# Transposed probabilities: four tiles in one round trip through the scratch tensor instead of two tiles in each of two

## The chip, the cores and the metric

The kernel runs on one core of one Trainium2 chip. The metric is the device time of one execution in microseconds. Three runs of the kernel before gave a median of 2397.24 us (2396.45 to 2406.7). Besides these there is one profiled execution with its trace.

Engines are named as in the profile: PE is TensorE (PEld its weight loads), DVE is VectorE, ACT is ScalarE, POOL is GpSimd, SP is SyncE, which here issues every DMA.

## The reference

The reference is a decoder of two layers on 16 sequences of 64 tokens with 512 features, in float32: self attention, cross attention and a feed-forward part per layer, each with a residual and a layer norm behind it. Three of these six parts are 32-head attentions with 8 key/value heads of size 128, and only they are touched by the change. Cut to what matters (the masks differ; the third takes keys and values from the context and normalises queries and keys by their root mean square):

```python
qg = q.reshape(B, Hkv, G, N, D)                       # G = 4 query heads share one key head
s = einsum('bhgnd,bhmd->bhgnm', qg, k) * scale + bias # 64 x 64 scores per sequence and head
p = softmax(s, axis=-1)
o = einsum('bhgnm,bhmd->bhgnd', p, v)                 # needs p with its keys on the partitions
x = layernorm(x + o.reshape(B, N, Hq * D) @ wo.T)
```

The other parts (a small linear cross attention, a feed-forward part with int4 weights, a mixture of low-rank experts) stay as they are.

## The kernel before

The 1024 tokens are 8 tiles of 128 rows (two sequences each). All matrix products are made in three passes, from a high and a low part of each operand (`mm3`, L263 to L265), so every tensor that goes into TensorE is split in two: ScalarE or GpSimd writes the high part, VectorE or GpSimd subtracts to get the low part.

`pe_attention` and its namesakes for the other engines run the three 32-head attentions as three stages, `attn0` (roughly the first 565 us of the profile), `attn1` (from 1123 us) and `xattn1` (up to 2353 us, the one with `rms`). A stage is a loop over the 8 key/value heads i. In each turn TensorE projects queries, keys and values of head i (12 units, `U_0` to `U_11`) and in between works off the attention of head i - 1. The order is a list of words written out by hand in `schedule` (L65); every engine walks the same list and does its own share of each word. A minus behind a word means the head before. The words:

- `U_n`: a projection unit, 12 matmuls of 512 columns on TensorE, its bank emptied by ScalarE (in `xattn1` VectorE copies key and value units, L777 and L778, and normalises keys, L789).
- `SC` scores of one pair of tiles, with the softmax on VectorE and ScalarE; GpSimd multiplies by the reciprocal sums (L961). A head has 4 such pairs, so 4 times 128 x 512 probabilities in `sc_sb`.
- `TR` transposes: VectorE turns the probabilities of one pair in blocks of 32 x 32 (L843) into `pq[:, pair % 2]`. The blocks themselves still have to change places between partitions. That is done by DMA: `move_out` (L461) writes `pq` in 4 pieces of 64 KB to the DRAM tensor `turned[pair % 2]`, `move_in` (L466) reads it back in one transfer of 256 KB to `pt[:, pair % 2]`.
- `PT` splits the result: ScalarE `pth` (L729), VectorE `ptl` (L868). Both wait for `move_in`, ScalarE directly.
- `PV` multiplies it with the values on TensorE (L608); ScalarE makes `oth` (L733) and VectorE `otl` (L874).
- `WS` splits a chunk of the output weights (ScalarE `woh` L740, VectorE `wol` L883), `WO` projects a tile of the output with them (12 matmuls) and VectorE adds it to `X` (L880). The first `WO` of a head needs the four chunks one after the other, one per group of three matmuls.
- `KT` and `SQ` (`xattn1` only) transpose the normalised keys (L586) and sum squares of queries.

An engine's instructions run in the order of its program, so a wait holds everything behind it on that engine. SyncE is such an engine too: in `sp_attention`, `step` issues for each head six loads of projection weights (`load_w`, into five slots of `raw`, each as soon as the slot's last content is split: for c = 0 to 3 that is WS of chunk c), four loads of output weights (`load_o`) and, between them at fixed places, `move_out` and `move_in` of pairs 2 and 3 of the head before and of pairs 0 and 1 of this head. GpSimd splits the projection weights (L945, L947) and in `xattn1` the values (L954, L956).

After the last head comes a tail, the list in the branch `if not project` (L76), without projections to fill in; there the layer norm begins.

## Time and profile before

| | |
|---|---|
| median of three runs | 2397.24 us (2396.45 to 2406.7) |
| profiled execution | 2401.77 us |
| its span, first to last instruction | 2400.0 us |
| granted TensorE clock, mean | 0.973 of full speed |
| PE busy | 2289.1 us, 95% |
| DVE, ACT, POOL busy | 1206.0, 780.5, 765.6 us |
| VectorE transposes (L843) | 96, mean 704 ns |
| DMA | 152.43 MB, mean 64 GB/s |

The busy times say which engine is close to being full, not what a change is worth: for that one has to read, in the stretch where the change lies, which wait ended last before TensorE went on. Starts in a timeline are in microseconds from the first instruction. The starts and ends of matmuls overlap, since they are pipelined; what matters is the distance from start to start. `x4` behind a row means that four like instructions stand in it, one behind the other.

### The profile page before, as it was taken

How to read it: one execution, taken by the hardware profiler on the slowest of the kernel's cores; microseconds unless marked ns; L12 is line 12 of the kernel's file. 1: busy time of each engine (PE TensorE's matmuls, PEld its weight loads, DVE VectorE, ACT ScalarE, POOL GpSimd, SP SyncE). 2: the span in 40 equal slices, each digit the busy share in tenths (PEclk: the TensorE clock that was granted, in tenths of full speed). 3: DMA queues.
4: the chain of work that ended last, by engine and by line, in shares of the span. 5: the costliest groups of instructions: out<-in, count | busy, mean ns of one | idle time of the engine just before them, and what ended most of it. 6: DMA issues, size and time to landing. Idle time of an engine off the chain costs nothing. (4 is left out here: it accounts for less than half of the span.)

```text
span 2400.0 us, 34599 instructions
## 1 busy us (share of the span) xinstructions
PE 2289.1 (95%) x12210; PEld 1833.6 (76%) x12210; DVE 1206.0 (50%) x2052; ACT 780.5 (33%) x1475; POOL 765.6 (32%) x709
## 2 busy tenths in 40 slices
PE   8999999997999989998999999998899999999989
PEld 6888888875555557886788888887788888888867
DVE  3445544447677633334444444556345454544456
ACT  2233223223677731222322223332232233323321
POOL 4122222203333335444222222211443433333233
PEclk9999999998999999999999999999889999999989
DMA  4222222211000113311221222121121212211120
GB/s 160 80 66 60 76 79 79 57 45 32 18 18 11 64 70 123 105 52 54 81 80 50 67 75 78 56 53 49 59 80 54 57 48 79 67 43 53 53 75 36
DMA packets 120546, 152.43 MB, mean 64 GB/s; under 512 B 16272, under 2 KB 67984, under 8 KB 119952
## 3 DMA queue, kind: packets, MB, share of 16 engines
q1 hardware_dynamic: 120464, 151.33, 21.5%
q8 instruction: 52, 0.85, 0.1%
q14 instruction: 30, 0.25, 0.0%
HBM read 124.02 MB, written 27.26 MB: 63 GB/s over the span
## 5 line engine op out<-in xcount | busy, mean ns | idle before, releaser
L263 PE MATMUL banks<-xTh,wh 128*128 128x512 f32 x1024 | 418.7, 409 | 8.8 <-DVE xTl L1887 7.4
L265 PE MATMUL banks<-xTh,wl 128*128 128x512 f32 x1024 | 404.7, 395 | 0.0
L264 PE MATMUL banks<-xTl,wh 128*128 128x512 f32 x1024 | 403.6, 394 | 0.0
L263 PE MATMUL banks<-woh,oth 128*128 128x512 f32 x768 | 315.6, 411 | 23.3 <-DVE otl L874 16.4
L264 PE MATMUL banks<-wol,oth 128*128 128x512 f32 x768 | 302.5, 394 | 0.0
L961 POOL TENSOR_TENSOR sc_sb<-sc_sb,rs 128x512 f32<-128x512 f32 x96 | 104.3, 1090 | 621.1 <-DVE rs L837 621.1
L265 PE MATMUL banks<-woh,otl 128*128 128x512 f32 x768 | 302.1, 393 | 0.0
L880 DVE TENSOR_TENSOR X<-banks,X 128x512 f32<-128x512 f32 x192 | 132.7, 691 | 324.3 <-PE banks L265 323.9
L693 ACT ACTIVATE q_sb<-banks 128x512 f32<-128x512 f32 x192 | 114.5, 597 | 400.6 <-PE banks L265 400.6
L263 PEld LDWEIGHTS banks<-xTh,wh 128*128 128x128 f32 x1024 | 195.6, 191 | 51.0 <-issue 9.2
L265 PEld LDWEIGHTS banks<-xTh,wl 128*128 128x128 f32 x1024 | 194.9, 190 | 44.0
L264 PEld LDWEIGHTS banks<-xTl,wh 128*128 128x128 f32 x1024 | 195.9, 191 | 37.3
L564 PEld LDWEIGHTS banks<-k_sb,q_sb 128*128 128x128 f32 x1536 | 191.0, 198 | 19.0 <-ACT q_sb L693 6.7
L874 DVE TENSOR_TENSOR otl<-banks,oth 128x512 fp32r<-128x512 f32 x192 | 123.6, 686 | 158.6 <-ACT oth L733 158.6
L564 PE MATMUL banks<-k_sb,q_sb 128*128 128x64 f32 x1536 | 191.4, 279 | 9.5 <-ACT q_sb L693 4.1
L263 PEld LDWEIGHTS banks<-woh,oth 128*128 128x128 f32 x768 | 146.2, 190 | 69.3 <-DVE otl L874 17.9
L947 POOL TENSOR_TENSOR wl<-raw,wh 128x512 fp32r<-128x512 f32 x144 | 193.4, 1343 | 12.0
L945 POOL TENSOR_SCALAR wh<-raw 128x512 fp32r<-128x512 f32 x144 | 91.0, 632 | 314.1 <-DMA raw<-in_a_in 163.7
L265 PEld LDWEIGHTS banks<-woh,otl 128*128 128x128 f32 x768 | 145.9, 190 | 32.4
L264 PEld LDWEIGHTS banks<-wol,oth 128*128 128x128 f32 x768 | 146.4, 191 | 26.3
L733 ACT ACTIVATE oth<-banks 128x512 fp32r<-128x512 f32 x192 | 104.3, 596 | 124.1 <-PE banks L608 124.1
L690 ACT ACTIVATE sq<-banks 128x512 f32<-128x512 f32 x64 | 38.3, 598 | 242.7 <-PE banks L265 242.7
(208 smaller groups left out, 4039.9 us busy)
## 6 DMA issues: line engine op xcount, KB each, us to landing
raw<-in_a_in SPq DMA_DIRECT2D x144, 256.0 KB, 2.9
raw<-in_a_out SPq DMA_DIRECT2D x96, 256.0 KB, 2.7
turned<-pq SPq DMA_DIRECT2D x384, 64.0 KB, 2.0
pt<-turned SPq DMA_DIRECT2D x96, 256.0 KB, 2.9
f_q<-in_f_q SPq DMA_DIRECT2D x21, 512.0 KB, 3.9
f_s<-in_f_s SPq DMA_DIRECT2D x21, 512.0 KB, 5.3
X<-in_x SPq DMA_DIRECT2D x1, 2048.0 KB, 10.5
x_craw<-in_ctx SPq DMA_DIRECT2D x8, 256.0 KB, 2.7
```

The costliest lines, as they stand in the source:

```text
L263: nc.tensor.matmul(out, w_hi, x_hi, start=start, stop=False)
L264: nc.tensor.matmul(out, w_hi, x_lo, start=False, stop=False)
L265: return nc.tensor.matmul(out, w_lo, x_hi, start=False, stop=stop)
L564: last = nc.tensor.matmul(pb[2][:, (4 * c + m) * S:(4 * c + m + 1) * S], q_sb[:, 4 * (pair % 2) + m, c * P:(c + 1) * P], k_sb[:, col:col + S],
L690: nc.scalar.activation(sq[:, :, g % 2 * S:(g % 2 + 1) * S], bank[:, :].rearrange("p (c s) -> p c s", c=8), ACT.Square).then_inc(A["q_sq"], 1)
L693: nc.scalar.activation(q_sb[:, :, g * S:(g + 1) * S], bank[:, :].rearrange("p (c s) -> p c s", c=8), ACT.Copy).then_inc(A["q_free" if st.r ...
L733: nc.scalar.activation(oth[:, n % 2, :, 64 * b:64 * b + 64], PVB[b][:, :].rearrange("p (c s) -> p c s", c=8), ACT.Copy).then_inc(A["o_hi"], 1)
L874: nc.vector.tensor_tensor(otl[:, n % 2, :, half], PVB[b][:, :].rearrange("p (c s) -> p c s", c=8), f32(oth[:, n % 2, :, half]), ALU.subtra ...
L880: nc.vector.tensor_tensor(xtile(n), bank[:, :], xtile(n), ALU.add).then_inc(A["x_added"], 1)
L945: nc.gpsimd.tensor_scalar(hi, src, 1.0, 0.0, ALU.mult, ALU.add).then_inc(A["w_hi"], 1)
L947: nc.gpsimd.tensor_tensor(lo, src, f32(hi), ALU.subtract).then_inc(A["w_ready"], 1)
L961: nc.gpsimd.tensor_tensor(rows, rows, spread_rows(rs[:, pair, :]), ALU.mult).then_inc(A["p_ready"], 1)
```

## The change

Pairs 0 and 1 now travel together, as half 0, and pairs 2 and 3 as half 1.

- `TR0` and `TR2` leave the lists; `TR1` and `TR3` make both transposes of their half back to back and then count once on `t_done`.
- `move_out` writes both buffers of `pq` in 4 pieces of 128 KB; `move_in` reads 512 KB into both buffers of `pt`.
- For half 1 SyncE issues `move_out` behind `load_w` 2 (before: behind `load_w` 1 for pair 2 and behind `load_w` 3 for pair 3) and `move_in` behind `load_w` 4 (before: behind 2 and 4). For half 0 `move_out` stands behind `load_o` 1 (`xattn1`: 2) and `move_in` one place further.
- One semaphore each instead of two for the pieces and for the return.

```diff
--- before.py
+++ after.py
@@ -68,13 +68,13 @@
 
 
     if rms:
-        ev = events("U_0 PT0- TR2- U_1 WS0- WS1- U_2 PV0- PT1- TR3- WS2- WS3- U_3 WO0- PV1- U_4 KT0 PT2- WO1- U_5 KT1 PV2- WO2- SQ0 "
-                    "U_6 PT3- U_7 WO3- SQ1 PV3- SC0 WO4- SC1 U_8 U_9 WO5- SQ2 TR0 U_10 U_11 TR1 WO6- SQ3 SC2 WO7- SC3")
+        ev = events("U_0 PT0- U_1 WS0- WS1- U_2 PV0- PT1- TR3- WS2- WS3- U_3 WO0- PV1- U_4 KT0 PT2- WO1- U_5 KT1 PV2- WO2- SQ0 "
+                    "U_6 PT3- U_7 WO3- SQ1 PV3- SC0 WO4- SC1 U_8 U_9 WO5- SQ2 U_10 U_11 TR1 WO6- SQ3 SC2 WO7- SC3")
     else:
-        ev = events("U_0 VT1- PT0- TR2- U_1 WS0- WS1- U_2 PV0- PT1- TR3- WS2- WS3- U_3 WO0- PV1- U_4 PT2- WO1- U_5 PV2- WO2- SC0 "
-                    "PT3- WO3- SC1 U_6 PV3- WO4- U_7 WO5- U_8 TR0 WO6- U_9 TR1 WO7- SC2 U_10 SC3 U_11 VT0")
+        ev = events("U_0 VT1- PT0- U_1 WS0- WS1- U_2 PV0- PT1- TR3- WS2- WS3- U_3 WO0- PV1- U_4 PT2- WO1- U_5 PV2- WO2- SC0 "
+                    "PT3- WO3- SC1 U_6 PV3- WO4- U_7 WO5- U_8 WO6- U_9 TR1 WO7- SC2 U_10 SC3 U_11 VT0")
     if not project:
-        return events("PT0- TR2- PV0- WO6-- " + ("" if rms else "VT1- ") + "PT1- TR3- WO7-- WS0- WS1- PV1- WS2- WS3- WO0- PT2- WO1- "
+        return events("PT0- PV0- WO6-- " + ("" if rms else "VT1- ") + "PT1- TR3- WO7-- WS0- WS1- PV1- WS2- WS3- WO0- PT2- WO1- "
                       "PV2- WO2- PT3- WO3- PV3- WO4- WO5- WO6- WO7-")
     if project == "last":
         return [e for e in ev if e[0] != "WO" or e[1] < 6]
@@ -293,7 +293,7 @@
         names = dict(
             proj_done=96, proj_free=96, sc_done=32,
             s_out=32, s_max=32, s_sub=32, exp_done=32, s_sum=32, s_rec=32, p_ready=32,
-            t_done=32, pt_hi=32, pt_ready=32,
+            t_done=16, pt_hi=32, pt_ready=32,
             pv_done=32, o_hi=64, o_ready=64,
             wo_done=64, x_added=64,
             wo_hi=32, wo_ready=32,
@@ -307,8 +307,8 @@
         ld_w = [sem(f"ld_w{c}") for c in range(6)]
         ld_o = [sem(f"ld_o{c}") for c in range(4)]
         ld_b = sem("ld_b")
-        pt_in = [sem(f"pt_in{n}") for n in range(2)]
-        pq_out = [sem(f"pq_out{n}") for n in range(2)]
+        pt_in = sem("pt_in")
+        pq_out = sem("pq_out")
         turned = nc.dram_tensor("turned", (2, P, 512), F32, kind="Internal").ap()
 
         xs = {n: sem("x_" + n) for n in (
@@ -419,7 +419,7 @@
 
         def pt_wait(eng, st, i, pair, more):
 
-            wait(eng, pt_in[pair % 2], 16 * (16 * st.index + 2 * i + pair // 2 + more))
+            wait(eng, pt_in, 16 * (16 * st.index + 2 * i + pair // 2 + more))
 
         def input_quarter(n):
 
@@ -454,16 +454,16 @@
                         sp.dma_start(bias[r, :, :], src.rearrange("p (c g s) -> p c g s", c=2, g=2)[:, :, h, :]
                                      ).then_inc(ld_b, 16)
 
-            def move_out(i, pair):
-                st.need(sp, "t_done", 4 * i + pair + 1)
-                rows = turned[pair % 2].rearrange("(bk j) (q n) -> q j bk n", bk=4, q=4)
+            def move_out(i, half):
+                st.need(sp, "t_done", 2 * i + half + 1)
+                rows = turned.rearrange("t (bk j) (q n) -> q j (t bk) n", bk=4, q=4)
                 for q in range(4):
-                    sp.dma_start(rows[q], pq[32 * q:32 * q + 32, pair % 2, :].rearrange("j (bk n) -> j bk n", bk=4)
-                                 ).then_inc(pq_out[pair % 2], 16)
-
-            def move_in(i, pair):
-                wait(sp, pq_out[pair % 2], 64 * (16 * st.index + 2 * i + pair // 2 + 1))
-                sp.dma_start(pt[:, pair % 2, :], turned[pair % 2]).then_inc(pt_in[pair % 2], 16)
+                    sp.dma_start(rows[q], pq[32 * q:32 * q + 32, :, :].rearrange("j t (bk n) -> j (t bk) n", bk=4)
+                                 ).then_inc(pq_out, 16)
+
+            def move_in(i, half):
+                wait(sp, pq_out, 64 * (16 * st.index + 2 * i + half + 1))
+                sp.dma_start(pt[:, :, :], turned.rearrange("t p n -> p t n")).then_inc(pt_in, 16)
 
             if st.before:
                 sp.wait_ge(*stage_end(st.before))
@@ -491,7 +491,7 @@
 
             def step(i, before, more):
 
-                first, second = (1, 2) if st.rms else (0, 1)
+                second = 2 if st.rms else 1
                 for c in range(5):
                     if more:
                         if c < 4:
@@ -499,20 +499,20 @@
                         else:
                             st.need(sp, "w_ready", 6 * i + 6)
                         load_w(i + 1, c, c)
-                    if before and c in (1, 3):
-                        move_out(i - 1, 2 + c // 2)
-                    if before and c in (2, 4):
-                        move_in(i - 1, 1 + c // 2)
+                    if before and c == 2:
+                        move_out(i - 1, 1)
+                    if before and c == 4:
+                        move_in(i - 1, 1)
                 for c in range(4):
                     if more:
                         st.need(sp, "w_ready", 6 * (i + 1) + c + 1)
                     else:
                         st.need(sp, "wo_ready", 4 * (i - 1) + c + 1)
                     load_o(i, c, c)
-                    if c in (second, second + 1):
-                        move_in(i, c - second)
-                    if c in (first, second):
-                        move_out(i, c - first)
+                    if c == second + 1:
+                        move_in(i, 0)
+                    if c == second:
+                        move_out(i, 0)
                 if more:
                     load_bias(i + 1)
                     st.need(sp, "w_ready", 6 * (i + 1) + 5)
@@ -522,9 +522,8 @@
             with sp.Fori(1, NKV - 1) as i:
                 step(i, True, True)
             step(NKV - 1, True, False)
-            for pair in (2, 3):
-                move_out(NKV - 1, pair)
-                move_in(NKV - 1, pair)
+            move_out(NKV - 1, 1)
+            move_in(NKV - 1, 1)
 
 
         def pe_attention(pe, st):
@@ -806,7 +805,7 @@
                 rows = sc_sb[:, pair, :, :]
                 b = bias[:, :, :].rearrange("p c (o s) -> p c o s", o=1).to_broadcast([P, 2, 4, S])
                 st.need(dve, "sc_done", 4 * i + pair + 1)
-                st.need(dve, "t_done", 4 * (i - 1) + pair + 1)
+                st.need(dve, "t_done", 2 * (i - 1) + pair // 2 + 1)
                 if st.per_head_bias:
                     dve.wait_ge(ld_b, 32 * (i + 2))
                 else:
@@ -836,13 +835,16 @@
                 st.need(dve, "s_sum", 4 * i + pair + 1)
                 nc.vector.reciprocal(rs[:, pair, :], ssum[:, pair, :]).then_inc(A["s_rec"], 1)
 
-            def transpose_probs(i, pair):
-
-                st.need(dve, "p_ready", 4 * i + pair + 1)
-                pt_wait(dve, st, i, pair, 0)
-                nc.vector.transpose(pq[:, pair % 2, :].rearrange("p (bk ct i) -> p ct bk i", bk=4, i=32),
-                                    sc_sb[:, pair, :, :].rearrange("p c s -> p (c s)").rearrange(
-                                        "p (ct bk i) -> p ct bk i", bk=4, i=32)).then_inc(A["t_done"], 1)
+            def transpose_probs(i, half):
+
+                pt_wait(dve, st, i, 2 * half, 0)
+                for n in range(2):
+                    pair = 2 * half + n
+                    st.need(dve, "p_ready", 4 * i + pair + 1)
+                    last = nc.vector.transpose(pq[:, n, :].rearrange("p (bk ct i) -> p ct bk i", bk=4, i=32),
+                                               sc_sb[:, pair, :, :].rearrange("p c s -> p (c s)").rearrange(
+                                                   "p (ct bk i) -> p ct bk i", bk=4, i=32))
+                last.then_inc(A["t_done"], 1)
 
             def run(i, events):
                 for kind, n, age in events:
@@ -862,7 +864,7 @@
                     elif kind == "SU":
                         sums(j, n)
                     elif kind == "TR":
-                        transpose_probs(j, n)
+                        transpose_probs(j, n // 2)
                     elif kind == "PT":
                         st.need(dve, "pt_hi", 4 * j + n + 1)
                         nc.vector.tensor_tensor(ptl[:, :], pt[:, n % 2, :], f32(pth[:, :]),
```

## Rows read from the trace of the kernel before

**Rows 1.** The page, busy us, share of the span and instructions of each engine.
```profile
PE 2289.1 (95%) x12210; PEld 1833.6 (76%) x12210; DVE 1206.0 (50%) x2052; ACT 780.5 (33%) x1475; POOL 765.6 (32%) x709
```

**Rows 2.** Windows of steady heads, stages one and three: stretch, length, busy us, clock.
```profile
100.00:510.00 410.00, 409.93 (x2183) 338.24 (x2182) 191.72 (x327) 113.71 (x205) 91.03 (x91) 1.00 0.24 67
...
1836.00:2240.00 404.00, 389.94 (x2451) 340.46 (x2450) 204.86 (x396) 120.83 (x277) 145.83 (x141) 1.00 0.21 59
```

**Rows 3.** TensorE's waits, whole kernel: us in total, times, longest.
```profile
PE banks L263 <- DVE otl L874: 16.4, 7, 2.8
...
PE banks L608 <- DVE ptl L868: 14.1, 5, 5.5
```

**Rows 4.** The page's DMA issues: count, KB each, median us from issue to landing.
```profile
turned<-pq SPq DMA_DIRECT2D x384, 64.0 KB, 2.0
...
pt<-turned SPq DMA_DIRECT2D x96, 256.0 KB, 2.9
...
f_q<-in_f_q SPq DMA_DIRECT2D x21, 512.0 KB, 3.9
...
f_s<-in_f_s SPq DMA_DIRECT2D x21, 512.0 KB, 5.3
```

**Rows 5.** Timeline of VectorE, stage one: start, duration, line, tiles.
```profile
336.72 0.70 DVE L843 STREAM_TRANSPOSE pq<-sc_sb 128x512 f32<-128x512 f32 x1
...
345.27 0.69 DVE L868 TENSOR_TENSOR ptl<-pt,pth 128x512 fp32r<-128x512 f32 x1 [2.17 <-ACT pth L729]
```

**Rows 6.** Timeline of VectorE, 337.5 to 338.2 us: WS2 alone.
```profile
337.35 1.16 DVE L883 TENSOR_TENSOR wol<-raw,woh 128x512 fp32r<-128x512 f32 x1
```

**Rows 7.** Timeline of GpSimd, 335 to 339 us.
```profile
336.21 1.74 POOL L947 TENSOR_TENSOR wl<-raw,wh 128x512 fp32r<-128x512 f32 x1
```

**Rows 8.** Timeline of TensorE, 338 to 350 us: third group of WO0, and PV2.
```profile
338.16 0.39 PE L265 MATMUL banks<-woh,otl 128*128 128x512 f32 x1
...
338.56 0.50 PE L263 MATMUL banks<-woh,oth 128*128 128x512 f32 x1
...
349.45 0.39 PE L608 MATMUL banks<-pth,vh 64*128 64x256 f32 x2
```

**Rows 9.** Timeline of SyncE's DMA issues, 338 to 345 us.
```profile
338.67 0.36 SPq L440 DMA_DIRECT2D raw<-in_a_in  x1
...
340.16 1.93 SPq L461 DMA_DIRECT2D turned<-pq  x4
...
344.08 0.34 SPq L466 DMA_DIRECT2D pt<-turned  x1
```

**Rows 10.** Timeline of ScalarE, 344 to 346 us.
```profile
344.61 0.62 ACT L729 ACTIVATE pth<-pt 128x512 fp32r<-128x512 f32 x1
```

**Rows 11.** Timeline of VectorE, stage three.
```profile
1847.25 0.70 DVE L843 STREAM_TRANSPOSE pq<-sc_sb 128x512 f32<-128x512 f32 x1
...
1856.24 1.25 DVE L883 TENSOR_TENSOR wol<-raw,woh 128x512 fp32r<-128x512 f32 x2
...
1866.28 0.98 DVE L789 TENSOR_SCALAR kst<-kst,rk 128x128 f32<-128x128 f32 x2
```

**Rows 12.** Timeline of TensorE, 1852 to 1869 us.
```profile
1855.15 0.50 PE L263 MATMUL banks<-woh,oth 128*128 128x512 f32 x1 [2.77 <-DVE otl L874]
...
1856.95 0.50 PE L263 MATMUL banks<-woh,oth 128*128 128x512 f32 x1
...
1868.20 0.60 PE L586 MATMUL banks<-ident,kst 128*128 128x128 f32 x4
```

**Rows 13.** Timeline of GpSimd, 1861 to 1869 us.
```profile
1867.27 1.28 POOL L956 TENSOR_TENSOR vl<-vst,vh 128x512 fp32r<-128x512 f32 x1
```

**Rows 14.** Timeline of SyncE's DMA issues, 1857 to 1865 us.
```profile
1857.06 0.36 SPq L440 DMA_DIRECT2D raw<-in_a_in  x1
```

**Rows 15.** Timeline of SyncE's DMA issues, tail of stage one.
```profile
539.16 0.34 SPq L466 DMA_DIRECT2D pt<-turned  x1
```

**Rows 16.** Timeline of VectorE, tail of stage one.
```profile
544.19 0.68 DVE L868 TENSOR_TENSOR ptl<-pt,pth 128x512 fp32r<-128x512 f32 x1
```

## The prediction

> **What bounds the kernel now.** I read the page's busy lines first, then TensorE's waits, then the busy time of two stretches, then the timelines around one head. TensorE is busy 2289.1 us, 95% [rows 1]. In the steady heads of the first attention stage it has nothing to give back: 409.93 of 410 us busy, and the second stage is the same program with the same picture. In the steady heads of the third, 14 of 404 us are idle [rows 2], before L263 on `otl` (16.4 us in 7 waits in the whole kernel) [rows 3]. So the transfers that the change merges are no bound; what counts is whether the new order makes TensorE wait. Waits on `ptl`, the far end of the changed chain, cost it 14.1 us in 5 places, with 5.5 the longest [rows 3], all in the tails of the stages, where few projections are left to fill in. SyncE, which issues the 384 pieces out and the 96 returns [rows 4], waits for events most of the time, so half of these issues gone buys nothing by itself.
>
> **Part 1, the second transpose in front of the weight split (first two stages).** TR2 stood after PT0, where VectorE next waits for ScalarE; taken out there, it gives TensorE nothing. It now runs behind TR3, and right behind that stands WS2. A transpose starts 0.63 us before what follows it (336.72 to 337.35) [rows 5, 6]. WS2 starts at 337.35 and takes 1.16 us, where two of its kind take 1.25 together in the third stage [rows 6, 11]. It ends as late as 338.51 because L947 on GpSimd runs until 337.95 beside it, for 1.74 us instead of the 1.28 of L956, which does the same work on another tile [rows 7, 13]. The transpose at 336.72 took its 0.70 us beside that L947 too, and I take the second one to do the same. It then fills the wait that WS2 has anyway: WS2 starts at 337.98, with L947 gone, takes 0.68 and ends at 338.66, 0.15 us later. TensorE already waits there: the third L263 of that output projection starts 0.40 us after a matmul of 0.39, though matmuls overlap elsewhere, and 0.05 us behind the end of WS2 [rows 8]. So 0.15 us is exposed in full. 11 heads of the two stages stand like this (0 to 5, without the very first, whose WO0 comes later): 1.7 us. Head 6 of each stage has no L947 beside it; there WS2 would end without delay at about 338.03 by this head's clock, and 0.61 later is 0.1 to 0.3 past its need, with 0.1 for the slower first matmul behind a wait (0.50 instead of 0.39): 0.7 us for the two. Bounds: 0 (the second transpose hidden) and 13 times 0.61, 7.9 us.
>
> Weighed beside it: the Trainium skill, "SBUF — State Buffer", Who interferes with whom, says that a VectorE instruction with two SBUF inputs and a GpSimd one that reads SBUF exclude each other wholly, and that one with a single SBUF input, outside the two-port modes, does not contend. By this rule, the trace agrees: 1.16 and 1.74 us are an undisturbed one and 0.46 to 0.5 each, and the transpose keeps its 0.70. Without the rule part 1 would be 7.9 us, with it 2.4.
>
> **Part 2, the same move in the third stage.** Here VectorE is in the chain. TR2 (1847.25) is followed back to back by the copies of the next projection unit, these by ScalarE's squares, WS0 and WS1, the next copies, and `otl` of PV0, for which TensorE waits 2.77 us before it starts WO0 at 1855.15 [rows 11, 12]. Without TR2 this comes 0.62 us earlier. But then follow `ptl`, two transposes instead of one, and WS2: its first half starts at 1856.24 again, and the third L263, at 1856.95 behind it today, stays there. Minus 0.62 and plus 0.62: 0. Bounds: minus 4.3 us (7 heads by 0.62, if WS2 did not hold the third L263) and plus 4.3.
>
> **Part 3, PT2 gets its data later.** Today PT2 (`pth` on ScalarE, 344.61) [rows 10] is not held by its data; they have been there for over 2 us. Now the pieces of pairs 2 and 3 leave together behind load_w 2, which waits for WS2. That load was issued 0.16 us behind WS2's end, at 338.67; now 338.82, and the first piece 0.4 later, behind the load's own 0.36: 339.22. From the first piece of pair 3 to the issue of its return passed 3.92 us (340.16 to 344.08) for 256 KB [rows 9]. Another 256 KB add 1.0, the difference of `f_q`'s 512 KB, landed after 3.9, and the return's 256 KB, landed after 2.9 [rows 4]. So the merged return is issued at 344.14; with `f_q`'s 3.9 it lands at 348.04. `pth` and `ptl` need 1.35 us (344.61 to 345.96) [rows 5, 10]: 349.39. TensorE comes to PV2 at 349.45 [rows 8], plus part 1's 0.15: 349.60. It is hidden, with 0.2 us to spare. Bounds: a landing 2.9 or 5.3 us (`f_s`) after issue, that is 1.2 to spare or 1.2 late; late counts in 12 heads. Behind PT2 on VectorE stands the X addition of WO1, needed by WO2 behind the whole of PV2: covered; on ScalarE nothing is due before U_5 ends.
>
> In the third stage: load_w at 1857.06 [rows 14], first piece 1857.46, return 1862.38, landed 1866.3 (1865.3 to 1867.7). PV2 comes behind L586 and is covered. But behind PT2 and the addition on VectorE stand the two L789 that normalise the last keys, today done at 1867.26; TensorE's transposes of these keys (L586) start at 1868.20, 0.9 us in hand [rows 11, 12]. `pth` would end at 1866.9, `ptl` at 1867.6 or a little after, the addition 0.6 later, and L789 meets L956 on GpSimd, which starts at 1867.27 and runs 1.28 us [rows 13]. Today the two L789, of 128x128 each, need 0.98 us beside other work of GpSimd, so they would be held until L956 ends. With the earliest landing the keys are ready near 1868.95, 0.75 late, with 1866.3 near 1869.55, 1.35 late. I take 1.0 us in 6 heads (0 to 5; head 6 has neither the loads in front nor GpSimd beside it): 6.0 us. Bounds 0 and 2.0 each, 12.
>
> **Part 4, the rest.** TR0 beside TR1: those pairs are read only in the next head, behind a further 10 us and more of projections; nothing there is late. The tails: the pieces leave right behind the transposes, 0.6 later than today. The return, today issued at 539.16 [rows 15], goes out near 540.3 with the larger pieces and lands at 544.2. `pth` and `ptl` then end near 545.5 instead of 544.87 [rows 16], and PV2, with a little in hand today, starts some 0.4 late: 0.8 us for the two tails of this kind; in the third stage the data come earlier against their reader. Bounds 0 and 3.
>
> **Sum.** 1.7 + 0.7 + 0 + 0 + 6.0 + 0.8 = 9.2 us. The profiled execution took 2401.77 us for a span of 2400.0, so it would take 2411.0; it lies 4.5 us above the median of 2397.24, and against that median the change gives 2406.4.
>
> **Rivals.**
> A, the slower side: PV2 waits for the merged return in the first two stages. It decides from a landing later than 348.2, 4.1 us behind its issue. For it: the return follows two 256 KB loads (load_w 3 and 4) and 512 KB in 512-byte rows into the same queue, and `f_s` took 5.3. Against it: `f_q` at 3.9, and the smaller returns, which land in 2.9 behind a load as well. Price: at 5.3 us 1.2 late in 12 heads, 14 us, and 1.8 in the third stage instead of 1.0, 5 us: 2425.
> B, no wait for the keys: L789 goes in before L956, or the return lands 1.5 us sooner. For it: the gap in which VectorE finds GpSimd between two instructions. Against: `ptl`, the addition and L789 would have to fit before 1867.27. 2406.4 - 6.0 = 2400.4.
> C, faster: the 0.62 us is gained at WO0 in the third stage and WS2 does not take it back, with B as well: 2396.1. Against: the third L263 starts right behind WS2 now, and WS2's own chain does not get shorter.
> That the transfers are not merged as said gets nothing: they are plain copies of strided rows.
>
> **Chances.** Forecast 0.48, A 0.27, B 0.20, C 0.05. A measurement of this kernel tells 0.5% from no change, 12 us: 2385 and 2409. Slower: A and the upper end of the forecast (0.06), 0.33. Faster: 0.03, what C may hide. Same: 0.64. The range goes from C to A: 2395 to 2425.
>
> **What the changed profile would show.** In a steady head of the first stages WS2 is about 0.7 us long and the third L263 waits 0.15 more; if 0.6, part 1 is four times its price. In the third stage the wait before WO0 falls from 2.8 to 2.2 us and the one at the third L263 grows by as much. The return is issued 5 us behind its first piece and lands 3.9 later; L586 waits for L789, 0.7 to 1.4 us, six times. A wait of L608 on `ptl` in steady heads would be rival A. A steady head that gets shorter would make the whole wrong.

## Result, and the profile after

The changed kernel takes 2429.53 us, the median of four runs (2424.98 to 2439.92), against 2396.84 (2395.8 to 2406.7) for the kernel before: a ratio of 1.0126, 95% interval 1.0097 to 1.0155. The forecast was 2406.4 us, with a range up to 2425; the kernel is slower than that. Ratios here and below are worked out over all runs of either kernel, so they differ a little from the quotient of the medians. The profiled execution took 2428.49 us for a span of 2426.7, 26.7 more than before. Its mean granted clock was 0.970 of full speed, before 0.973.

The busy line of the page (busy time, share of the span, instructions), which answers to [rows 1]:

```profile
PE 2299.8 (95%) x12210; PEld 1838.8 (76%) x12210; DVE 1199.7 (49%) x2052; ACT 783.8 (32%) x1475; POOL 763.7 (31%) x709
```

TensorE did the same 12210 matmuls and was busy 10.7 us longer, though no matmul was added; the other 16 us of the 26.7 are idle time. What ended its idle time (us in all, number of waits, the longest), which answers to [rows 3]:

```profile
PE banks L607 <- DVE ptl L870: 19.4, 13, 5.5
PE banks L263 <- DVE otl L876: 12.6, 7, 2.2
PE banks L263 <- DVE wol L885: 9.7, 14, 0.7
PE banks L585 <- DVE kst L788: 6.2, 6, 1.5
PE banks L354 <- DVE X L346: 4.1, 4, 1.9
```

Waits on `ptl` were 5 and are 13. Six waits on `kst`, the keys, are new, and so are most of those on `wol`: 6 waits of 3.9 us together before. The first matmul behind a wait is slower as well, so the growths given below are up to 0.16 us larger per wait than the idle time: 7.2 us for the keys, where these lines have 6.2. The transfers themselves are merged as the diff says (count, KB each, median us from issue to landing; before in [rows 4]):

```profile
turned<-pq SPq DMA_DIRECT2D x192, 128.0 KB, 2.5
pt<-turned SPq DMA_DIRECT2D x48, 512.0 KB, 3.8
```

**Where the 26.7 us are.** I set the start of each of the 12210 matmuls of one trace against its counterpart in the other, and read the growth of the distance from place to place. The first attention stage holds 2.0, the second 6.1, the third 17.0; what lies between and behind them gives 1.0 back; the first 36 us, where the first weights are loaded, cost 2.6, and a second profile of the kernel before has 3.3 there as well, so that is taken as chance. By kind, in us (growth at a matmul that runs at another clock in one of the two traces is the clock's, growth at one behind another wait is the wait's):

| | predicted | in the two profiles |
|---|---|---|
| third L263 of WO0, first two stages | 2.4 | 2.1 |
| WO0 in the third stage | 0 | 0.4 |
| PV2 waits for the data, steady heads | 0 | 4.2 |
| keys (L585) in the third stage | 6.0 | 7.2 |
| tails | 0.8 | 4.0 |
| TensorE at half clock in the third stage | not in the sum | 6.3 |
| start; between and behind the stages; the rest of the stages | 0 | 2.6 - 1.0 + 0.9 |

The half clock: added up over the third attention stage, the clock was granted at half speed for 64.9 us instead of 51.2. In the steady heads 2 to 6 of that stage (stretch, length, then busy time and count of PE, PEld, DVE, ACT, POOL, then the granted clock, DMA share and GB/s), before:

```profile
1839.50:2232.00 392.50, 378.44 (x2363) 329.31 (x2362) 196.30 (x380) 117.81 (x270) 144.78 (x140) 1.00 0.22 60
```

and after:

```profile
1849.40:2255.90 406.50, 387.64 (x2362) 335.53 (x2361) 195.80 (x380) 119.38 (x270) 143.66 (x140) 0.98 0.21 58
```

Five heads are 14.0 us longer. 4.8 us of that is idle time of PE (18.9 instead of 14.1), 9.2 is busy time with the same matmuls, most of it because the clock falls four times (a fall is a stretch of half clock; they last 3.4 or 6.8 us here). Such a fall, and an undisturbed stretch close to it, in the kernel after:

```profile
1897.90:1901.30 3.40, 3.40 (x14) 3.01 (x14) 2.59 (x5) 0.13 (x1) 1.94 (x3) 0.50 0.00 0
1890.90:1894.30 3.40, 3.40 (x18) 2.81 (x17) 0.32 (x1) 1.09 (x2) 0.00 (x0) 1.00 0.00 0
```

TensorE is busy through both and waits for nobody, but in the first it runs at 0.50, that is 1.2 instead of 2.4 GHz. A list of waits does not show this at all; only the clock column does.

**One head, as the prediction went through it.** SyncE in the head of [rows 9] (start, duration, instruction), in the kernel after:

```profile
342.19 0.33 SPq L440 DMA_DIRECT2D raw<-in_a_in  x1
342.67 1.98 SPq L461 DMA_DIRECT2D turned<-pq  x4
344.90 1.27 SPq L440 DMA_DIRECT2D raw<-in_a_in  x2
347.25 0.38 SPq L466 DMA_DIRECT2D pt<-turned  x1
```

This head lies 3 us later than before. The return goes out 4.58 us behind the first piece, where the prediction had 4.92. On VectorE, the last subtraction of PT1, the two transposes and WS2 with WS3:

```profile
339.56 0.68 DVE L870 TENSOR_TENSOR ptl<-pt,pth 128x512 fp32r<-128x512 f32 x1
340.16 1.30 DVE L844 STREAM_TRANSPOSE pq<-sc_sb 128x512 f32<-128x512 f32 x2
341.38 1.25 DVE L885 TENSOR_TENSOR wol<-raw,woh 128x512 fp32r<-128x512 f32 x2
```

WS2 no longer meets GpSimd: two of its kind take 1.25 us together, where one took 1.16 [rows 6]. That is the cover that part 1 counted on. The reader of the returned data is ScalarE:

```profile
351.28 0.63 ACT L728 ACTIVATE pth<-pt 128x512 fp32r<-128x512 f32 x1 [3.00 <-DMA pt<-turned]
```

It starts when the transfer has landed, 4.0 us behind its issue, after 3.0 us of waiting. `ptl` is ready about 352.6, and PV2 starts at 353.01: this head escapes by 0.4 us. Others don't. Over the 24 heads the return of half 1 lands 3.4 to 5.3 us behind its issue, median 4.05, and in the first two stages PV2 waits in seven steady heads (3.7 us of waits, 4.2 with the slower matmuls behind them), for instance:

```profile
285.29 0.39 PE L607 MATMUL banks<-pth,vh 64*128 64x256 f32 x2 [0.40 <-DVE ptl L870]
```

In the third stage the keys, TensorE first, then VectorE:

```profile
1879.77 0.65 PE L585 MATMUL banks<-ident,kst 128*128 128x128 f32 x4 [1.51 <-DVE kst L788]
```

```profile
1877.95 0.70 DVE L870 TENSOR_TENSOR ptl<-pt,pth 128x512 fp32r<-128x512 f32 x1 [6.15 <-ACT pth L728]
1878.57 0.68 DVE L882 TENSOR_TENSOR X<-banks,X 128x512 f32<-128x512 f32 x1
1879.17 0.47 DVE L788 TENSOR_SCALAR kst<-kst,rk 128x128 f32<-128x128 f32 x2
```

VectorE stands 6.15 us idle in front of `ptl`, the last link behind the transfer, and the two normalisations that TensorE waits for are queued behind it though their own data were there. In this head the return landed 5.3 us behind its issue. In two others of the six it was `ptl` that took long, beside GpSimd's `vl` (L958, 2038.10 to 2039.39):

```profile
2038.19 1.75 DVE L870 TENSOR_TENSOR ptl<-pt,pth 128x512 fp32r<-128x512 f32 x1 [5.09 <-ACT pth L728]
```

These three waits are 1.4 to 1.5 us. In the other three the first normalisation took 0.71 us and ended with GpSimd's L958, and TensorE waited 0.5 to 0.7.

The third stage's tail has a path of its own. Behind the last return SyncE issues the loads for the next part of the decoder (`g_raw`). The first of them goes out 12.5 us after PV0's start in that tail and lands 4.3 us behind its issue; in the kernel before these were 11.1 and 3.0 us. GpSimd waits for it, and only when it has split these weights does it make `rstd`, the root of the layer norm. VectorE's L346 now waits for `rstd`, and did not before:

```profile
2350.48 0.41 SPq L1676 DMA_DIRECT2D g_raw<-in_g_gate  x1
```

```profile
2354.83 1.05 POOL L1691 TENSOR_SCALAR g_h<-g_raw 128x552 fp32r<-128x552 f32 x1 [15.96 <-DMA g_raw<-in_g_gate]
```

```profile
2359.86 0.84 DVE L346 TENSOR_SCALAR X<-X,mv,rstd 128x512 f32<-128x512 f32 x1 [2.37 <-POOL rstd L341]
```

### The profile page after: what moved, and what is told of

It is laid out like the page before. It is cut to its first block and busy times, and to the rows that moved or that the text cites. A ratio compares the mean times of both kernels' runs of the same rounds, so it can differ in the third digit from the quotient of the medians.

```text
span 2426.7 us, 34327 instructions
## 1 busy us (share of the span) xinstructions
PE 2299.8 (95%) x12210; PEld 1838.8 (76%) x12210; DVE 1199.7 (49%) x2052; ACT 783.8 (32%) x1475; POOL 763.7 (31%) x709
## 3 DMA queue, kind: packets, MB, share of 16 engines
q1 hardware_dynamic: 116624, 151.32, 20.6%
## 5 line engine op out<-in xcount | busy, mean ns | idle before, releaser
L263 PE MATMUL banks<-xTh,wh 128*128 128x512 f32 x1024 | 418.0, 408 | 9.5 <-DVE xTl L1889 8.0
L263 PE MATMUL banks<-woh,oth 128*128 128x512 f32 x768 | 318.7, 415 | 25.5 <-DVE otl L876 12.6
L263 PEld LDWEIGHTS banks<-xTh,wh 128*128 128x128 f32 x1024 | 194.8, 190 | 52.3 <-issue 9.3
L563 PEld LDWEIGHTS banks<-k_sb,q_sb 128*128 128x128 f32 x1536 | 196.6, 203 | 18.5 <-ACT q_sb L692 6.7
L563 PE MATMUL banks<-k_sb,q_sb 128*128 128x64 f32 x1536 | 197.3, 285 | 8.9 <-ACT q_sb L692 4.1
L263 PEld LDWEIGHTS banks<-woh,oth 128*128 128x128 f32 x768 | 147.7, 192 | 72.8 <-DVE wol L885 19.4
L947 POOL TENSOR_SCALAR wh<-raw 128x512 fp32r<-128x512 f32 x144 | 90.9, 631 | 314.3 <-DMA raw<-in_a_in 164.5
L870 DVE TENSOR_TENSOR ptl<-pt,pth 128x512 fp32r<-128x512 f32 x96 | 71.9, 749 | 151.5 <-ACT pth L728 151.5
## 6 DMA issues: line engine op xcount, KB each, us to landing
X<-in_x SPq DMA_DIRECT2D x1, 2048.0 KB, 10.4
```

The lines of the kernel that those rows point to most:

```text
L263: nc.tensor.matmul(out, w_hi, x_hi, start=start, stop=False)
L563: last = nc.tensor.matmul(pb[2][:, (4 * c + m) * S:(4 * c + m + 1) * S], q_sb[:, 4 * (pair % 2) + m, c * P:(c + 1) * P], k_sb[:, col:col + S],
L870: nc.vector.tensor_tensor(ptl[:, :], pt[:, n % 2, :], f32(pth[:, :]), ALU.subtract).then_inc(A["pt_ready"], 1)
L947: nc.gpsimd.tensor_scalar(hi, src, 1.0, 0.0, ALU.mult, ALU.add).then_inc(A["w_hi"], 1)
```

## Experiments

### Which half of the change costs the time

**e1_dma_only.** The transfers of after with the transposes where they stood before; `move_out` waits for both of its half.

```diff
-                st.need(sp, "t_done", 2 * i + half + 1)
+                st.need(sp, "t_done", 4 * i + 2 * half + 2)
```

> Transfers merged as in the changed kernel, but the four transposes stay at their old places in the lists (TR2 behind PT0, TR0 behind U_8), so only SyncE's part of the change is made. Theory R (the merged return of pairs 2 and 3 comes late): the waits of L608 on ptl in steady heads and of the key transposes on L789 stay as in the changed kernel, 5 to 6 us and about 7 us, with the stretches at half clock in the third stage; only the 2 us in front of WS2 go, about 2427. Theory T (the loss comes from two transposes in a row on VectorE): within 3 us of before, about 2398.

Measured: 2423.54 us against 2398.65, ratio 1.0089 (1.0063 to 1.0115). The waits show the two mechanisms of the merged return (PV2 and the keys), with `wol` near what it was, and `otl` too (16.8 us):

```profile
PE banks L607 <- DVE ptl L867: 17.8, 9, 5.5
PE banks L585 <- DVE kst L788: 5.4, 6, 1.5
PE banks L263 <- DVE wol L882: 4.7, 8, 0.7
```

**e2_tr_only.** The other half: transposes in couples, transfers per pair as before.

```diff
+                        transpose_probs(j, n - 1)
                         transpose_probs(j, n)
```

> Transposes two by two at TR1 and TR3 as in the changed kernel, transfers per pair (64 KB pieces, 256 KB returns) at the places of before. Theory R: only the wait of WO0's third group on wol is longer, 2 us in all, no wait for the keys: about 2399. Theory T: nearly the whole loss, 2420 or more.

Measured: 2403.85 us, ratio 1.0013 (0.9998 to 1.0028).

```profile
PE banks L608 <- DVE ptl L869: 13.7, 4, 5.5
PE banks L263 <- DVE wol L884: 9.0, 13, 0.7
```

There are no waits for the keys and none of PV2 in steady heads. `wol` grows as in part 1 and in the third stage, where `otl` falls by as much (12.3 us instead of 16.4). The wait on `X` at L354 in the third tail grows too, from 1.9 to 5.2 us in all, without a merged transfer: here as well the loads of `g_raw` go out later, 15.1 us after PV0's start in that tail instead of 11.1. So the transposes cost a few us at most; most of the loss is in the transfers.

**e3_half0_only.** Only pairs 0 and 1 travel together, transposes and transfers; half 1 as before.

```diff
-                    if c in (second, second + 1):
-                        move_in(i, c - second)
-                    if c in (first, second):
-                        move_out(i, c - first)
+                    if c == second + 1:
+                        in_pairs(i)
+                    if c == second:
+                        out_pairs(i)
...
+                        if n == 1:
+                            transpose_probs(j, 0)
```

(`out_pairs` sends 4 pieces of 128 KB, `in_pairs` brings 512 KB back.)

> Only pairs 0 and 1 merged (transposes and transfers), pairs 2 and 3 as before. Theory R: no change, 2397 within 3 us, since the reader of half 0 comes 9 us and more after its landing. A rival by which merging costs wherever it is done (longer use of the queue in front of the weight loads): a loss of a third or more, 2407 and up.

Measured: 2401.58 us, ratio 1.0001 (0.9985 to 1.0018). Half 0 costs nothing that can be measured, as the forecast had it. The loss is in half 1.

### Which wait of half 1

**e4_keys_first.** After, but in the third stage VectorE does `ptl` of PT2 behind the keys instead of ahead of them.

```diff
+        if st.rms and project and ("PT", 2, 1) in both:
+            both.remove(("PT", 2, 1))
+            both.insert(both.index(("U_", 5, 0)) + 1, ("PT", 2, 1))
```

> The changed kernel with one thing moved: in the third stage VectorE does the low part ptl of PT2 behind the copies and key normalisation of U_5, so that the keys no longer stand behind the return. Theory R with the clock as its consequence: the 7.2 us of waits before the key transposes go, and with them the half-clock stretches added in the third stage (13.7 us of them, worth 6.3 us), a wait of PV2 on ptl of 0 to 0.3 us per head in their place: 12 us below the changed kernel, about 2417. If the half-clock stretches have another cause, only 6 to 7 us below it, about 2423.

Measured: 2415.06 us against 2398.65, ratio 1.0073 (1.0044 to 1.0101). No wait at L585 is left, `ptl` waits are

```profile
PE banks L607 <- DVE ptl L870: 19.9, 18, 5.5
```

and the third stage is at half clock for 41 us instead of 64.9. The median is 14 us under that of after (9 to 13 by the ratios, against either set of runs of after), where the key waits were 7: that speaks for a slower clock that comes with them. The four runs spread from 2406.6 to 2422.6, and the profile is the fastest of them, so its 41 us are the low end; e7 tests the same from the other side.

**e5_out_first.** After, with the pieces of half 1 sent ahead of `load_w` 2.

```diff
-                    if before and c == 2:
+                    if before and c == 1:
                         move_out(i - 1, 1)
```

> The changed kernel, but SyncE issues the pieces of pairs 2 and 3 in front of load_w 2 instead of behind it, so they leave when the transposes end and do not wait for WS2. Theory R (lateness of the return in front of its reader): pieces and return about 1.2 us earlier; the steady waits of L608 on ptl (5.6 us) nearly all go, the waits for the keys (7.2 us) fall to 4 or 5, since L789 is still held by GpSimd's L956. About 2418. If the queue's load decides instead (the same bytes in the same stretch), the return lands no earlier and nothing changes, 2429.

Measured: 2417.39 us against 2398.77, ratio 1.0081 (1.0061 to 1.0101). SyncE, and ScalarE's reader, in the head shown above:

```profile
338.94 1.85 SPq L461 DMA_DIRECT2D turned<-pq  x4
341.05 1.58 SPq L440 DMA_DIRECT2D raw<-in_a_in  x3
343.04 0.38 SPq L466 DMA_DIRECT2D pt<-turned  x1
```

```profile
347.97 0.63 ACT L728 ACTIVATE pth<-pt 128x512 fp32r<-128x512 f32 x1 [2.27 <-DMA pt<-turned]
```

The pieces leave as the transposes end, and the return is out 1.7 us sooner by this head's clock. But three loads of 256 KB now stand right in front of it, and it takes 4.9 us instead of 4.0 to land: half the gain is lost in the queue. The PV2 waits of steady heads are gone, those of the keys are 2.8 us (a growth of 3.6): they are all of the kind that ends with GpSimd's L958.

**e6_split_return.** After, with the return in two transfers of 256 KB; PT2 waits for the first alone.

```diff
-                sp.dma_start(pt[:, :, :], turned.rearrange("t p n -> p t n")).then_inc(pt_in, 16)
+                for n in range(2):
+                    sp.dma_start(pt[:, n, :], turned[n]).then_inc(pt_in[n], 16)
```

> The changed kernel, but the return of 512 KB is two returns of 256 KB with a semaphore each, issued one behind the other at the same place; PT2 needs only the first. Theory R with the size of the return as its cause: the first half lands 1 us or more sooner, the steady waits of L608 on ptl fall below 1.5 us (from 5.6), those for the keys to about 5: 2421. If the place of the return is all that counts, no change, 2429.

Measured: 2419.31 us, ratio 1.0088 (1.0073 to 1.0103). The first return lands 3.3 us behind its issue in the median (2.7 to 4.1).

```profile
PE banks L608 <- DVE ptl L872: 13.7, 4, 5.5
PE banks L586 <- DVE kst L789: 4.3, 6, 1.5
```

What the size of the return costs is PV2's waits, which are gone from the steady heads; the keys stay late, by less: five of the six waits are 0.5 to 0.6 us, held by GpSimd.

**e7_key_wait_alone.** The kernel before, with nothing of the change, and the wait for the keys made by work: two spare subtractions on VectorE ahead of `ptl` of PT2 in the third stage.

```diff
+                            for k in range(2):
+                                nc.vector.tensor_tensor(spare[:, k, :], pt[:, 0, :], f32(pth[:, :]), ALU.subtract)
```

> The kernel before, with transfers and transposes untouched; in the third stage VectorE makes two further subtractions of 128x512 into a spare tile in front of the ptl of PT2, except in the tail, which pushes the key normalisation L789 back by 1.3 us, as the late return does. It is there to see whether the clock follows such waits. If waits before the key transposes (expected: 6 of about 0.9 us, 5 us) bring half-clock stretches with them, the third stage has 60 us or more of them instead of 51 and the kernel is 8 to 12 us slower than before, 2407. If the half clock has another cause, 5 us slower, 2402, with 41 to 51 us of it.

Measured: 2419.01 us, ratio 1.0095 (1.0075 to 1.0116).

```profile
PE banks L587 <- DVE kst L790: 7.8, 6, 1.3
```

8.7 us of added waits (7.8 of idle time and the slower matmuls behind it) cost 20.2 us in the median. In its profile, the fastest of the four runs, the half clock of the third stage is 68.3 us and costs 7.3. So the key wait alone brings the clock's part too, without a merged transfer.

**e10_three_mends.** After with e4, e5 and e6 together.

```diff
-                    if before and c == 2:
+                    if before and c == 1:
...
+                for n in range(2):
+                    sp.dma_start(pt[:, n, :], turned[n]).then_inc(pt_in[n], 16)
...
+                    both.insert(both.index(("U_", 5, 0)) + 1, ("PT", 2, 1))
```

> The changed kernel with the three mends together: pieces of pairs 2 and 3 issued in front of load_w 2, the return in two halves, and ptl of PT2 behind the key normalisation in the third stage. Theory R: no steady wait on ptl and none for the keys; what is left is the 2 us in front of WS2 and 1 to 3 us in the tails, about 2400. If more than 6 us remain above before, the change has a further cost not found yet.

Measured: 2407.57 us against 2403.84, ratio 1.0014 (0.9995 to 1.0032).

```profile
PE banks L608 <- DVE ptl L872: 15.4, 9, 5.5
PE banks L263 <- DVE wol L887: 10.5, 20, 0.7
```

No key wait, 44 us of half clock. With the three places mended the change is no different from before that can be measured: they carry the loss. It is no gain either; the waits on `wol` and in the third tail are still there.

### Is it the clock

**v1_order.** Meant as a gain: the kernel before, in the third stage TR2 behind U_2 and TR3 behind WS3.

```diff
-U_0 PT0- TR2- U_1 WS0- WS1- U_2 PV0- PT1- TR3- WS2- WS3- U_3
+U_0 PT0- U_1 WS0- WS1- U_2 TR2- PV0- PT1- WS2- WS3- TR3- U_3
```

> The kernel before with only its order of the third stage changed: TR2 behind the copies of U_2 (VectorE is idle there for 1.29 us) instead of behind PT0, and TR3 behind WS3 instead of in front of WS2. By the reading of the chain of VectorE the wait before WO0 shrinks by 0.6 us and that before its third group by 0.3 to 0.4 in 7 heads, 6 to 7 us in all: 2391. If TensorE waits for ScalarE's oth in any case, no change.

Measured: 2417.84 us against 2398.77, ratio 1.0079 (1.0063 to 1.0094): 19 us slower. Its waits fell as meant, before WO0

```profile
PE banks L263 <- DVE otl L874: 12.1, 6, 2.2
```

from 16.4 [rows 3], 5.9 us less in all with those at the third L263. A head without a fall would take 77.6 us (an estimate: the 78.5 of before less 0.85; none of heads 2 to 6 is without one). But heads 2 to 6:

```profile
1836.40:2239.60 403.20, 392.79 (x2362) 342.36 (x2362) 195.40 (x380) 118.26 (x270) 145.55 (x140) 0.96 0.22 59
```

Idle time 10.4 us instead of 14.1, and the clock 0.96 instead of 1.00: seven falls, 34 us of half clock there. Less waiting, more time. This profile, too, is the fastest of its six runs.

**e8_pad_06.** The kernel before with one short spare reduction on VectorE in each head of the third stage, ahead of `otl` of PV0, to make the wait before WO0 0.6 us longer.

```diff
+                                for k in range(1):
+                                    nc.vector.tensor_reduce(spare[:, k, :], PVB[0][:, :].rearrange("p (c s) -> p c s", c=8), AX_X, ALU.max)
```

> The kernel before, with one further reduction of 128x512 on VectorE in front of the otl of PV0 in the third stage, which makes the wait before WO0 and so each head about 0.6 us longer (79.1 instead of 78.5 us) and touches nothing else. Theory C (which weak stretches of a head lose the clock depends on the length of a head; at 78.5 us heads 2 to 6 go free): falls of the clock reappear in heads 2 to 6, two or more, 4 us of waits plus 6 us or more of half clock, about 2409. Theory W (the clock falls where waits get longer, in proportion): 4.3 us and a little more, 2402 to 2404.

Measured: 2429.94 us against 2403.84, ratio 1.0093 (1.0063 to 1.0123).

```profile
PE banks L264 <- DVE otl L878: 20.6, 7, 3.4
```

```profile
1835.70:2261.60 425.90, 409.25 (x2363) 353.44 (x2362) 200.42 (x386) 118.67 (x271) 143.92 (x140) 0.92 0.20 56
```

4.2 us more of waits, 26 us in the median. In each of the heads 2 to 6 the clock falls three times, 15 falls, 68 us of half clock; its third stage pays some 23 us more than that of before for matmuls at half clock. Each of the five waits before WO0, now 3.2 to 3.5 us, is followed by a fall at once. What a fall looks like from inside, TensorE behind the wait before WO0 (start, duration):

```profile
1852.03 0.50 PE L264 MATMUL banks<-woh,oth 128*128 128x512 f32 x1 [3.45 <-DVE otl L878]
1852.61 0.45 PE L266 MATMUL banks<-woh,otl 128*128 128x512 f32 x1
1852.85 0.63 PE L264 MATMUL banks<-woh,oth 128*128 128x512 f32 x1
1853.27 0.63 PE L265 MATMUL banks<-wol,oth 128*128 128x512 f32 x1
1853.70 0.63 PE L266 MATMUL banks<-woh,otl 128*128 128x512 f32 x1
```

From 1852.85 on the starts are 0.43 us apart instead of 0.23.

**e9_pad_34.** The same with five reductions and a half, to lengthen the wait by 3.4 us.

```diff
+                                for k in range(5):
...
+                                nc.vector.tensor_reduce(spare[:, 5, 0:4], PVB[0][:, 0:256].rearrange("p (c s) -> p c s", c=4), AX_X, ALU.max)
```

> The same with five and a half such reductions, about 3.4 us longer heads (81.9 us), the length by which half-clock stretches are multiples in the records. Theory C: the heads are again of a length that goes free, 24 us of waits and no added half clock in heads 2 to 6: 2421. Theory W: the longest waits of all the kernels, 24 us and more half clock than in any, 2435 or more.

Measured: 2460.45 us, ratio 1.0236 (1.0205 to 1.0268).

```profile
PE banks L264 <- DVE otl L879: 39.6, 7, 6.1
```

```profile
1841.40:2285.10 443.70, 413.76 (x2363) 357.29 (x2362) 213.26 (x411) 118.57 (x271) 144.45 (x140) 0.90 0.18 53
```

The expectation that heads of this length would go free again and lose nothing but the 23 us of waits fell: there are 15 falls here too, and one of them begins within each of the five waits of 6 us. So the run changes two things at once, the length of a head and that of the wait, and does not tell whether the length of a head matters.

**v2_ws2_early.** Meant as a gain on before: in the first two stages WS2 ahead of PT1.

```diff
-PV0- PT1- TR3- WS2- WS3- U_3
+PV0- WS2- PT1- TR3- WS3- U_3
```

> The kernel before with one word moved: in the first two stages WS2 stands in front of PT1 and TR3, so that VectorE makes the third chunk of output weights before GpSimd's L947 takes the shared path, and TensorE's third group of WO0 does not wait. It gives back 0.17 us of wait and 0.11 us of a slower first matmul in 11 heads: 3 us, 2394. If ScalarE's woh of that chunk then comes too late for it, no change.

Measured: 2409.86 us against 2403.84, ratio 1.0016 (0.9998 to 1.0034), where 2394 was expected. A miss; the waits on `wol` grew from 6 to 18:

```profile
PE banks L263 <- DVE wol L883: 10.2, 18, 0.7
```

Its third stage is that of before, untouched, and has three falls in head 2, where the first profile of before has none in heads 2 to 6.

### How far the profiles themselves differ

**c1_before_again and c2_after_again.** Both kernels once more, unchanged.

```diff
 (no edit)
```

> The kernel before, unchanged, profiled a second time. If its half clock in the third stage (51 us) is a property of the kernel, 41 to 55 us again and the same waits; if it is chance, anything up to 70 us, with the time moving along by half of the difference.

> The changed kernel, unchanged, profiled a second time. The waits of TensorE on ptl (5 to 6 us in steady heads) and for the keys (7 us) should come again within 1 us. The half clock of the third stage, 65 us in the first profile, comes again within 5 us if it belongs to the change, and falls to the 41 to 51 us of before if it was chance. Time near 2429 us, ratio 1.012.

Measured: before 2406.02 us (2397.13 to 2412.78) against 2400.13, ratio 1.0006 (0.9984 to 1.0028); after 2428.37 us (2419.7 to 2433.05), ratio 1.0111 (1.0082 to 1.014). The result holds. The new profile of before took 2412.78 us, and heads 2 to 6 of its third stage

```profile
1843.60:2242.60 399.00, 384.82 (x2364) 333.95 (x2362) 196.49 (x380) 118.25 (x270) 145.16 (x140) 0.98 0.21 59
```

show three falls where the first profile has none, all in head 6, with hardly a wait more. So the same program can lose the clock by chance, and 6 us of one profile's distance are within that chance. One profile's count of falls is weak evidence therefore; the last part below goes over all runs. The new profile of after has the key waits (5.5 us), `ptl` 18.3 us in 13 waits, `wol` 9.1 in 14, and four falls in heads 2 to 6 (20 us of half clock); it is the fastest of its six runs.

## Why the prediction was wrong

**What held.** Part 1: 2.1 us instead of 2.4, and WS2 free of GpSimd. A steady head paid 0.1 us and not 0.15, and a single wait of 0.7 us (at 1188 us) made up for it, so the sum is closer than its parts. The Trainium skill, "SBUF — State Buffer", Who interferes with whom, says that a VectorE instruction with two SBUF inputs contends with a GpSimd one that reads SBUF, by an exclusive lock. The trace agrees: WS2 took 1.16 us beside L947, and two of them take 1.25 together without it. Part 2: over seven heads the wait before WO0 in the third stage fell by 3.8 us and the one at the third L263 grew by 4.2, nearly the nothing of the forecast:

```profile
1864.41 0.50 PE L263 MATMUL banks<-woh,oth 128*128 128x512 f32 x1 [2.17 <-DVE otl L876]
1866.80 0.50 PE L263 MATMUL banks<-woh,oth 128*128 128x512 f32 x1 [0.71 <-DVE wol L885]
```

Against 2.77 and 0.12 before [rows 12]. The key waits of part 3: 7.2 and, in the second profile, 5.5 us, instead of 6.0, six and five times, in the place named. That the sum is so near is in part luck. Each was to be 0.75 to 1.35 us late, held by GpSimd; three were held so and cost 0.7 to 0.8, three came later, by a late landing or by `ptl` itself beside GpSimd, and cost 1.6 to 1.7. Half 0 at nothing: e3.

**Step that failed, 1: "with `f_q`'s 3.9 it lands at 348.04 ... hidden, with 0.2 us to spare".** The median was nearly right, 4.05 us, and the merged return even went out 0.3 us sooner than worked out. But a margin of 0.2 us was held against one median, while landings spread from 3.4 to 5.3 us, and only the late ones count. Which heads are late changes from profile to profile: the return at 1193.6 us took 5.3 us to land, the same one in the second profile 4.2. Seven of the steady heads were late, for 4.2 us in all. That is rival A's mechanism at a third of its price; A had put every head at the worst landing. e6 shows that the size of the return does it (first half lands 3.3 us behind issue, waits gone), e5 that what stands in front of it on SyncE adds to it (4.9 to 5.7 us in the steady heads of the first two stages behind three loads, 3.7 to 5.3 behind two). The Trainium skill, "DMA: Bandwidth & Descriptors", Anatomy of one DMA, gives 2.0 us plus the bytes at 436 GB/s for GpSimd's queue; an estimate by it for 512 KB is 3.2 us, and these returns on SyncE's queue never came below 3.4.

**Step that failed, 2: the tails, 0.8 us, "in the third stage the data come earlier against their reader".** In the tails of the first two stages PV2 came 0.8 and 0.6 later, where 0.4 each was forecast. The third stage's tail lost 2.6. Of that 0.5 is at PV3, and this wait is 0.4 to 0.9 us in kernels with an untouched tail as well, so it may be chance. 2.1 is at L354 in the layer norm, which waits on `X` (4.1 us in 4 waits, 1.9 in 1 before), and what comes late there is not the probabilities: SyncE's loads of `g_raw` are later, GpSimd waits for them, and `rstd` stands behind that, as the rows above show. The prediction followed the readers of the moved transfer and not what stands behind it on SyncE. e2, with the transposes alone, has the same wait and more of it. 4.0 instead of 0.8, beyond the bound of 3 that was given.

**Step that failed, 3: the sum, "1.7 + 0.7 + 0 + 0 + 6.0 + 0.8".** It added waits and left out TensorE's clock. The steady heads of the third stage stood at full clock [rows 2], and I took that for a given. The profile after pays 6.3 us for it in the third stage. v1, e7 and e8 show the term without the merged transfers: 5.9 us of waits less and 19 us slower; 8.7 more and 20 slower; 4.2 more and 26 slower. In e4, where the key waits go, the clock's part goes with them (41 us of half clock). No rival had this in it. With the landings and tails as measured the sum would have been 16.6 us, 9.2 + 4.2 + 3.2; the profiles are 26.7 apart and the medians 28 to 33.

The runs without a profile confirm it, for each has its mean granted clock on record. The span times one minus that clock is an estimate of what the run lost to the clock. It is a little high: for the 13.7 us of half clock that the profile of after has more in the third stage it gives 6.9, where the matmuls pay 6.3. Means over all runs, in us above the kernel before measured beside it:

| kernel | longer by | of it clock | the rest |
|---|---|---|---|
| after, again (c2) | 24.7 | 9.6 | 15.1 |
| e1 | 22.2 | 11.3 | 10.9 |
| e2 | 2.7 | -2.1 | 4.7 |
| e4 | 14.0 | 3.8 | 10.2 |
| e5 | 19.6 | 13.2 | 6.3 |
| e6 | 20.6 | 9.6 | 11.0 |
| e7 | 21.8 | 13.9 | 7.9 |
| e8 | 24.7 | 23.9 | 0.8 |
| v1 | 17.6 | 26.1 | -8.5 |
| e10 | 3.2 | -3.3 | 6.5 |

So the rest of after is near the 16.6 of the mended sum, and about 10 us on top are the clock. In v1 and e8 nearly all of the loss is clock by this estimate. In e10 6.5 us other than clock are left, and its runs lost a little less to the clock than those of before. The spread of the kernel before is clock too: its 70 runs beside the experiments take 2395.0 to 2412.4 us at a mean clock of 0.978 to 0.969, and without the estimated loss they lie between 2336 and 2346.

**How it falls.** In heads 2 to 6 of the third stage the falls come at the same three places of a head in every kernel: 15 to 18 us into it, around the wait before WO0, and 45 to 49 and 72 to 79 us into it (52 and 83 in e9, whose wait is 3.4 us longer). At the last two TensorE does not wait. There it has just made the sums of squares, 16 matmuls one column wide that take 1.84 us, and is at scores 64 columns wide or just past them. The same matmuls stand in every head, also where no fall comes. Falls in heads 2 to 6, by the clock column of one profile each:

| kernel | falls | | kernel | falls |
|---|---|---|---|---|
| before, again | 0, 3 | | e5 | 2 |
| after, again | 4, 4 | | e6 | 3 |
| e1 | 5 | | e7 | 6 |
| e2, e3 | 0 | | v1 | 7 |
| e4, e10 | 1 | | e8, e9 | 15 |
| v2 | 3 | | | |

Heads without a fall take 78.2 to 78.9 us in before, e2, e3, e4 and e10, which nearly keep the clock, but also in v2 and in the second profile of before, which have three falls each. The kernels with four falls and more have heads shorter (v1, 77.6 by the estimate) or longer (79.3 to 80 in after, e1 and e7; e8 and e9 have none free of a fall) than that. So it is not the amount of waiting that decides. What else does is not settled: that the length of a head does was argued, and e9, which was to test it, spoke neither for it nor against it. The difference between the medians (28 to 33 us) and that between the two first profiles (26.7) is within the spread of the runs.

## What to carry to other kernels

A transfer that must be back in time is to be held against the latest landing in the trace and not the median, above all when two transfers with 2 us to spare are merged into one with 0.2. Before an engine's queue is given a longer wait, look at what stands behind the waiting instruction: in e4, moving one subtraction behind two ready ones brought back some 9 to 14 us. The same holds for SyncE: loads for the next part that stand behind a moved return can be what a tail waits for. And where TensorE is nearly full, read the clock column of the steady stretch beside the waits, for every kernel, and over several runs: here a shift of 0.6 us per head cost 26 us, and 5.9 us of waits won cost 19.

## What the hardware showed that I had not expected

The granted clock falls to 0.50 in stretches where TensorE is busy without a gap (3.40 of 3.40 us at 1897.9), at places with narrow matmuls; a shift of 0.6 us per head made it 15 falls in five heads (e8), and the unchanged kernel has 0 or 3. The starts of 512-column matmuls go from 0.23 to 0.43 us apart. SyncE's time for an issue does not follow the size: 0.33 us for 256 KB, 0.38 for 512 KB, 0.5 for each of the four pieces of 128 KB. A transfer of 512 KB behind three of 256 KB on the same queue took 4.9 us to land in a head where it took 4.0 behind two.
